# Attention scores from two float32r parts on half-height array tiles, with a new order inside the group

## The reference

```python
x = x + lru(layernorm(x))
z = layernorm(x)
h = z + attention(rmsnorm(z), wq, wk, wv, wo)   # 16 heads of 8, 1024 keys, no mask
h = h + moe(rmsnorm(h), gate, w1, w2, w3)       # 8 experts, best 2
x = x + h
```

## Time and profile before

| | |
|---|---|
| times of three runs | 1325.18, 1336.45, 1334.33 us; median 1334.33 |
| span of the profiled execution | 1326.4 us (the page gives no own time beside it; the lowest run is 1.2 us below this span) |
| mean granted TensorE clock | 0.951 of full |
| PE busy | 1187.2 us (90%) |
| DVE busy | 1033.9 us (78%) |
| ACT busy | 721.0 us (54%) |
| POOL busy | 293.1 us (22%) |
| DMA | 34.14 MB, 26 GB/s over the span |

### The profile page before, as it was taken

How to read it: one execution, slowest core, us unless ns; L and a number is a source line. 1 busy time by engine, 2 the same in 40 slices (tenths; PEclk the granted TensorE clock), 3 DMA queues, 4 the chain that set the end, 5 groups by cost and what they waited for, 6 DMA issues and landing times.

```text
span 1326.4 us, 26291 instructions
## 1 busy us (share of the span) xinstructions
PE 1187.2 (90%) x6720; PEld 583.9 (44%) x6720; DVE 1033.9 (78%) x2390; ACT 721.0 (54%) x1330; POOL 293.1 (22%) x154
## 2 busy tenths in 40 slices
PE   0266769999998999999998998999998999999998
PEld 0145522332332332332332332233335898888887
DVE  5977768888887887887887887789844677777675
ACT  1022322776776776776776776677785333333332
POOL 8133114222312222222122132132221101110100
PEclk9778866999998999999999999899999999999999
DMA  5002250011011011011011011011000000000000
GB/s 178 0 20 60 61 122 0 1 37 38 7 30 37 0 36 37 0 36 37 0 36 38 0 36 37 0 36 36 1 1 1 9 2 8 8 8 8 8 2 15
DMA packets 19748, 34.14 MB, mean 26 GB/s; under 512 B 4417, under 2 KB 13889, under 8 KB 16961
## 3 DMA queue, kind: packets, MB, share of 16 engines
q1 hardware_dynamic: 17456, 32.52, 10.7%
q10 hardware_dynamic: 2192, 0.66, 0.2%
HBM read 24.78 MB, written 8.39 MB: 25 GB/s over the span
## 4 chain that ended last, share of the span: by engine, by line
PE 78%; DVE 10%; issue 6%; DMA 3%; SPq 1%; ACT 1%; POOL 1%; DVEq 0%; POOLq 0%; ACTq 0%
PE ps L923 18%; PE ps L976 16%; PE ps L966 15%; PE ps L1126 13%; PE ps L1114 9%; DMA qpack<-q_parts 2%; PE ps L911 2%; DVE smax L670 2%; SPq L238 1%; DVE wk L624 1%; DMA xacc<-x 1%; PE ps L984 1%; PE ps L995 1%; PE ps L899 1%; POOL qpack L293 1%
## 5 line engine op out<-in xcount | busy, mean ns | idle before, releaser
L670 DVE TENSOR_REDUCE smax<-ps 128x1 f32<-128x512 f32 x1024 | 654.1, 686 | 104.9 <-PE ps L923 77.7
L462 ACT ACTIVATE prob<-ps 128x512 f32<-128x512 f32 x1024 | 537.3, 600 | 223.3 <-PE ps L966 200.4
L923 PE MATMUL ps<-kpack,qpack 96*128 96x512 bf16 x1024 | 365.4, 397 | 32.2 <-DVE smax L670 28.3
L966 PE MATMUL ps<-qpack,kpack 96*128 96x512 bf16 x1024 | 350.5, 385 | 1.5 <-ACT prob L462 1.5
L976 PE MATMUL ps<-prob,vpad 128*32 128x512 f32 x2048 | 278.0, 615 | 0.1
L923 PEld LDWEIGHTS ps<-kpack,qpack 96*128 96x128 bf16 x1024 | 100.2, 98 | 372.7 <-DVE smax L670 296.0
L293 POOL TENSOR_TENSOR qpack<-mtr,mdiag 12x2048 bf16<-12x2048 bf16 x32 | 129.9, 4058 | 585.8 <-ACT mtr L455 585.8
L1126 PE MATMUL ps<-split_parts 128*128 (+1 forms) x768 | 208.7, 407 | 0.0
L519 ACT ACTIVATE prob<-ps 128x512 f32<-128x512 f32 x128 | 76.6, 599 | 182.4 <-PE ps L1126 181.4
L851 DVE TENSOR_TENSOR prob<-ps,prob 128x512 f32<-128x512 f32 x128 | 87.9, 691 | 85.3 <-PE ps L1126 72.8
L1126 PEld LDWEIGHTS ps<-split_parts 128*128 128x128 f32 x768 | 135.0, 189 | 22.3
(11 more groups left out here) (154 smaller groups left out, 665.0 us busy)
## 6 DMA issues: line engine op xcount, KB each, us to landing
kpack<-k_parts SPq DMA_DIRECT2D x48, 192.0 KB
qpack<-q_parts SPq DMA_DIRECT2D x144, 64.0 KB
w<-w_t SPq DMA_DIRECT2D x3, 1024.0 KB, 10.1
q_parts<-qk SPq DMA_DIRECT2D x48, 64.0 KB, 1.6
k_parts<-qk SPq DMA_DIRECT2D x48, 64.0 KB, 1.6
xacc<-x SPq DMA_DIRECT2D x4, 512.0 KB, 7.9
out<-xacc SPq DMA_DIRECT2D x8, 256.0 KB, 2.3
gam<-gamma_row ACTq DMA_DIRECT2D x1, 64.0 KB, 5.5
```

Of the source, the lines that this page charges most:

```text
L462: act.activation(prob[:, v % RING, :], bank(3 + v % 3), ACT.Exp).then_inc(exp_done, 1)
L670: dve.tensor_reduce(smax[:, half, w // 2, w % 2:w % 2 + 1], bank(6 + u % 2 if opening else u % 3), AX_X, ALU.max).then_inc(s_max, 1)
L923: pe.matmul(bank(6 + u % 2 if opening else u % 3), qpack[:, slot, head, q0:q0 + P], kpack[:, slot, head, kh * 512:(kh + 1) * 512], start=T ...
L966: pe.matmul(bank(3 + v % 3), kpack[:, slot, head, kt * P:(kt + 1) * P], qpack[:, slot, head, half * HALF:(half + 1) * HALF], start=True, s ...
```

## The change

- q and k are split in two float32r parts (`PARTS = 2`) instead of three bf16 parts: ACT writes the high part straight from PSUM, DVE the rest as (PSUM times scale minus high), also from PSUM. Four cross products are 32 contraction rows; 2 rows hold the maxima: 34 partitions.
- Heads of even number lie on partitions 0 to 33, those of odd number on 64 to 97. A row *pair* is two matmuls, one of each half, into two neighbouring banks; one reduction takes the maxima of both. Pairs alternate between banks 0, 1 and 2, 3. The turned output takes one position of this rotation (O), the turned maxima one of the column rotation (banks 4 to 6). Values are in bank 7.
- In a group: both row pairs, four columns, values of the group before, then (where due) output turn and maxima turn.
- Maxima are split in two steps of float32r with nothing between them, turned by one transpose, and placed by two small DMAs on SP's queue instead of by POOL. POOL's clear becomes two memsets.
- Loads of a quad: 4 for k, 16 for q; 8 of the latter already after half the columns of the quad that held the slot.
- `front` staging of the first block uses banks 2 and 3; PE waits for the split before it overwrites the banks of q and k.

```diff
-PARTS = 3
-MROWS = PARTS * (HALF // P)
-PAIR0 = 24
-ROWS = PAIR0 + PARTS * PARTS * HD
+PARTS = 2
+CROSS = PARTS * PARTS * HD
+ROWS = CROSS + PARTS
+ODD = 64
+        def row_banks(pos):
+            return 2 * (pos % 2)
+        def col_bank(pos):
+            return 4 + pos % 3
...
 (sync: loop)
-                    sp.wait_ge(st_done, i * (2 * UNITS) + (slot + 1) * UNITS)
-                    load_pack(2 * i + 2 + slot, slot)
+                    sp.wait_ge(col_free, base + (M_OWN + 1))
+                    place_maxima(slot, 1)
+                    sp.wait_ge(col_full, base + (col_pos(JOB - 1) + 1))
+                    load_q(n, slot, 0)
+                    sp.wait_ge(col_free, base + (M_NEXT + 1))
+                    place_maxima(1 - slot, 0)
+                    sp.wait_ge(col_full, base + (col_pos(UNITS - 1) + 1))
+                    load_k(n, slot)
+                    load_q(n, slot, 1)
...
 (scalar: projections)
-                    act.activation(full, bank(2 + 2 * w, 2), ACT.Copy, scale=(scale, 1.0)[w]).then_inc(qk_saved, 1)
-                    act.activation(qk3[:, w, 0, :], full, ACT.Copy).then_inc(hi_ready, 1)
-                    act.activation(qk3[:, w, 1, :], (q_rest, k_rest)[w], ACT.Copy).then_inc(mid_ready, 1)
+                    act.activation(qk2[:, w, 0, :], bank(2 + 2 * w, 2), ACT.Copy,
+                                   scale=(scale, 1.0)[w]).then_inc(hi_ready, 1)
...
 (vector)
-                    dve.tensor_reduce(smax[:, half, w // 2, w % 2:w % 2 + 1], bank(6 + u % 2 if opening else u % 3), AX_X,
-                                      ALU.max).then_inc(s_max, 1)
+                    dve.tensor_reduce(smax[:, half, :, pair, qt, kh], ps[:, first:first + 2, :], AX_X,
+                                      ALU.max).then_inc(row_free, 1)
...
 (tensor: rows; `pos` is the place in the rotation)
+                    pe.wait_ge(row_free, base + (pos - 1))
+                for par in range(2):
+                    r = par * ODD
+                    ins = pe.matmul(bank(first + par), qpack[r:r + ROWS, slot, half, pair, qt * P:(qt + 1) * P],
+                                    kpack[r:r + ROWS, slot, pair, kh * HALF:(kh + 1) * HALF], start=True, stop=True)
+                ins.then_inc(row_full, 1)
...
 (tensor: columns)
-                    pe.wait_ge(exp_done, base + (2 + max(v - 2, 0)))
+                        pe.wait_ge(col_free, base + (pos - 2))
+                    pe.matmul(bank(col_bank(pos)), kpack[r:r + ROWS, slot, head // 2, kt * P:(kt + 1) * P],
+                              qpack[r:r + ROWS, slot, half, head // 2, :],
+                              start=True, stop=True).then_inc(col_full, 1)
...
 (tensor: turn of the output)
+                pe.wait_ge(row_free, row_item - 1)
                 for t in range(4):
+                    ins = pe.transpose(ps[:, o_bank, t * P:(t + 1) * P], oT[:, t * P:(t + 1) * P], ident[:, :])
+                ins.then_inc(row_full, 1)
...
 (tensor: group)
-                rows(0, 1)
-                score_cols(4 * g, 4 * g + 2, slot, units)
-                rows(1, 3)
-                score_cols(4 * g + 2, 4 * g + 3, slot, units)
-                rows(3, 4)
-                (turn_o, turn_maxima where due)
-                score_cols(4 * g + 3, 4 * g + 4, slot, units)
-                weigh_values(g - 1, slot, units)
+                rows(0)
+                rows(1)
+                score_cols(4 * g, 4 * g + 4, slot, cols, not has_next)
+                weigh_values(g - 1, slot, cols, not has_next)
+                (turn_o, turn_maxima where due)
```

More of the change, by code:

```diff
@@ L275, in _ @@
[L275 to L283, removed]
@@ L687, in _ @@
             norm_a(chain(0), B - 1)
-            dve.sem_inc(s_max, 4)
-            split_qk(B - 1, between=lambda: maxima(0, AHEAD, 0, opening=True))
+            split_qk(B - 1)
             assert count[0] == start + B * PER_BATCH, count[0]
             start += B * PER_BATCH
-            dve.sem_inc(o_done, 1)
             dve.sem_inc(hid_done, 2)
             dve.sem_inc(added, 2)
-            def split_maxima(job, half, units, before, first=False, beside=None):
-                done = [0]
-                def step(ins):
-                    ins.then_inc(dve_self, 1)
-                    if beside:
-                        maxima(beside[0] + done[0], beside[0] + done[0] + 1, beside[1])
-                    done[0] += 1
-                    dve.wait_ge(dve_self, before + done[0])
-                dve.wait_ge(s_max, units + 4)
-                if not first:
-                    dve.wait_ge(m_turned, job)
-                negated, rest = (nmax[:, i, :].rearrange("p (h t) -> p h t", h=HQ) for i in range(2))
-                step(dve.tensor_reduce(nmax[:, 0, :], smax[:, half, :, :], AX_X, ALU.max, negate=True))
-                step(dve.tensor_copy(mpart[:, :, 0, :], negated))
-                step(dve.tensor_tensor(rest, negated, mpart[:, :, 0, :], ALU.subtract))
-                step(dve.tensor_copy(mpart[:, :, 1, :], rest))
-                dve.tensor_tensor(mpart[:, :, 2, :], rest, mpart[:, :, 1, :], ALU.subtract).then_inc(m_split, 1)
@@ L723, in finish_o @@
+            def finish_o(quad, half, full, o_bank, before):
+                dve.wait_ge(row_full, full)
+                o = bank(o_bank).rearrange("p (g c) -> p g c", c=VW)
                 dve.reciprocal(rden[:, :], o[:, :, HD]).then_inc(dve_self, 1)
@@ L794, in first_front @@
                 assert count[0] == PER_BLOCK, count[0]
-            PER_QUAD = 10
-            maxima(AHEAD, JOB, 0, opening=True)
-            split_maxima(0, 0, JOB, start, first=True)
-            maxima(JOB, UNITS - LAG + 4 * START, 0)
-            start += 4
+            PER_QUAD = 6
+            maxima(0, 16, 0, opening=True)
+            split_maxima(0, 16, start)
+            maxima(16, PAIRS - 2, 0, opening=True)
+            start += 2
             def dve_quad(i, slot, last):
-                units = i * (2 * UNITS) + slot * UNITS
-                job, quad = 4 * i + 2 * slot, 2 * i + slot
+                base = i * (2 * ROW_ITEMS) + slot * ROW_ITEMS
+                quad = 2 * i + slot
@@ L805, in dve_quad @@
                 own = i * (2 * PER_QUAD) + (slot * PER_QUAD + start)
-                maxima(UNITS - LAG + 4 * START, UNITS, units)
-                following = units + UNITS
-                split_maxima(job + 1, 1, following, own, beside=None if last else (0, following))
+                following = base + ROW_ITEMS
+                maxima(PAIRS - 2, PAIRS, base)
+                split_maxima(1, base + (pair_pos(PAIRS - 1) + 1), own)
                 if not last:
-                    maxima(4, 28, following)
@@ L811, in dve_quad @@
-                finish_o(quad, 0, job, own + 4)
-                if not last:
-                    maxima(28, JOB, following)
-                    split_maxima(job + 2, 0, units + (UNITS + JOB), own + 5, beside=(JOB, following))
-                    maxima(JOB + 4, UNITS - LAG + 4 * START, following)
-                    finish_o(quad, 1, job + 1, own + 9)
-                else:
-                    first_front(own + 5)
-                    finish_o(quad, 1, job + 1, own + (5 + PER_BLOCK))
+                    maxima(0, 14, following)
@@ L896, in first_half @@
                 pe.wait_ge(uT_saved, b + 1)
+                if not first:
+                    pe.wait_ge(lo_ready, b * 2)
                 for i in range(2):
@@ L913, in product_y, with score_rows @@
                 ins.then_inc(y_done, 1)
[L915 to L925 removed]
+            def score_rows(p, slot, base, opening=False):
+                pos = pair_pos(p, opening)
+                half, pair, qt, kh = p // 16, p % 16 // 8, p % 8 // 2, p % 2
+                first = (6 - 2 * (p % 2)) if opening and p < 16 else row_banks(pos)
+                if not opening or p >= 2:
+                    pe.wait_ge(row_free, base + (pos - 1))
+                for par in range(2):
+                    r = par * ODD
+                    ins = pe.matmul(bank(first + par), qpack[r:r + ROWS, slot, half, pair, qt * P:(qt + 1) * P],
+                                    kpack[r:r + ROWS, slot, pair, kh * HALF:(kh + 1) * HALF], start=True, stop=True)
+                ins.then_inc(row_full, 1)
             def second_half(b, has_next):
@@ L951, in second_half @@
                     pe.wait_ge(v_saved, b + 1)
-            first_half(0)
+            first_half(0, first=True)
             product_y(0)
@@ new lines, in group @@
+                rows(0)
+                rows(1)
+                score_cols(4 * g, 4 * g + 4, slot, cols, not has_next)
+                if g == 0:
+                    if not opening:
+                        weigh_values(15, 1 - slot, cols - COL_ITEMS)
+                else:
+                    if g == 1:
+                        pe.wait_ge(vpad_in, quad + 1)
+                    if g % 8 == 1 and not (opening and g == 1):
+                        pe.wait_ge(o_saved, job + g // 8)
```

(1 more changed line is left out.)

388 lines of the change are left out of this document (208 added, 180 removed).

## The result

The changed kernel takes 1715.1 us (median of four runs, 1699.8 to 1716.2) against 1331.9 us before: 1.282 times as long, 95% interval 1.274 to 1.290. I had forecast 1362 us. The direction was right, the size and its cause were not.

What follows compares the result with a forecast made beforehand. PE was taken as the bound, DVE close. Terms +22 + 1 + 20 - 6 - 3.5 - 7 = +26.5, say +28 us, put on the 1334.3 us median: 1362 us; forecast 1345 to 1390, range 1322 to 1410.

Steps and rivals of the forecast that it cites:

- rival 4: TensorE's clock falls with idle time: +1.8 us a group over a fifth of the groups, about 1450 us; chance 0.03.
- My argument against the rival: Old kernel's last quad: groups of 2.40 us, idle share like the one expected, kept matmul spacing at 0.22.
- The group at 2.4 GHz: Plain attention group: 2.40 + 0.46 + 0.07 = 2.93 us against 2.84, +22 us over 244 groups.
- The chain: Column 0, exponential 0.44 us later, column 3 after 0.64, values after 0.32, next column 0 after 1.00: 2.40 us every group.
- 0.07 for loads: Weight loads on PE, after the values and at column 3, not wholly hidden: 0.07 us a group.
- Row pairs: Row matmuls of a group: the two halves run at the same time, 0.46 us, bounds 0.43 and 0.93.
- rival 1: Row halves do not run together, or their loads go one after the other: 1477 or 1438 us; chance 0.14.
- Maxima: DVE's two reductions of 1024 a group: 2.4 to 2.5 us, under PE's time, costed at nothing.
- Loads: PE's waits for loads at the end of a quad, 3.5 us in all before, go: -3.5 us.
- The turned output: Output turn in the row rotation: PE waits for DVE's division, 0.65 us about 31 times, +20 us.
- The turned maxima: Four transposes become one after the values: -0.2 us x 31 = -6 us, bounds 0 and -10.
- Opening: Before the first columns: 16 paired reductions replace 28, start 0.4 us earlier; -7 us, first columns near 211 us.

Runs made afterwards that it cites:

- the padded kernel: The changed kernel with all score matmuls over 64 contraction rows instead of 34, added rows zeros in q and ones in k: 1384.8 us, 1.040 of before.
- experiment 3: Changed kernel, score matmuls over 64 contraction rows instead of 34 (zeros in q, ones in k), order untouched: 1384.8 us, 1.040 of before.
- experiment 4: Kernel before (bf16, 96 rows) with only the order in a group changed, so that PE waits: 1397.3 us, 1.049 of before.
- experiment 8: Kernel before, order and bf16 kept, score matmuls over the first 34 of 96 contraction rows, output not the reference's: 1610 and 1686 us.
- experiment 2: Changed kernel with the values of the group before moved in front of column 3: 1591 and 1593 us, 1645 in two other runs; 1.195 of before.
- experiment 1: Changed kernel with alternating order: row pair, columns 0 and 1, row pair, columns 2 and 3, values: 1458 and 1521 us, no ratio given.

## Why the prediction was wrong, step by step

**The clock** was the step that failed. I had it as rival 4 with a chance of 0.03, about 1450 us, over a fifth of the groups, and brought on by idle time. The sum itself put the change from 96 to 34 contraction rows at nothing, without a reason. The runs show that this change cost most: its price is the difference to the padded kernel, the same list of instructions, 1715 - 1385 = **330 us** of the 383 lost, with a group of 5.00 us at the lower level instead of my 4.7. At 5.00 - 3.16 = 1.84 us a group, 330 us are about 180 of the 256 groups; this is an estimate. My argument against the rival, that the last quad of the old kernel kept its clock with the same idle share, was right about the waits (experiments 3 and 4), but those matmuls had 96 rows. At one level of the clock the narrow matmuls show no difference: at 2.4 GHz four row matmuls take 0.58 us over 34 rows and over 64 alike (604.61 - 604.03).

Idle time is not without effect. In the kernel before, PE stood still for 3.92 us at a turn of the loop, and the clock went down (stretches as above, then the first row unit after the standstill):

```profile
420.00:425.00 5.00, 1.25 (x6) 0.39 (x4) 0.71 (x2) 1.55 (x3) 0.00 (x0) 0.91 0.12 21
425.00:430.00 5.00, 4.83 (x15) 1.12 (x16) 2.94 (x8) 1.47 (x4) 0.00 (x0) 0.50 0.00 2
430.00:435.00 5.00, 5.00 (x32) 1.52 (x30) 4.37 (x10) 3.30 (x7) 0.00 (x0) 0.91 0.00 0
```

```profile
425.17 0.61 PE L923 MATMUL ps<-kpack,qpack 96*128 96x512 bf16 x1 [3.92 <-DVE smax L670]
```

With 96 rows it was back up soon after 430 us. In experiment 8, the same kernel over 34 rows, it went down behind a standstill of the same kind (PE busy for 2.2 us of 350 to 355) and stayed down until about 530.

**The group at 2.4 GHz.** Forecast 2.93 us, measured 3.16. The chain is the one I gave, column 3 waits in every group, but three terms were too small: rows 0.58 for 0.46, column 0 to its exponential 0.51 for 0.44, column 3 to the values 0.42 for 0.32. Exponential to column 3 (0.65) and the values (1.00) were right. I had allowed 0.07 for loads; the gap behind column 3 grew by 0.10, and its load takes 0.18 us there. That the load causes it was not tested.

**Row pairs** run together (rival 1 false). **Maxima**: the new reduction takes 1.22 us, DVE idle 0.6 to 0.8 us a group; right, and costs nothing. **Loads**: in the changed kernel PE waits for none any more; right.

**The turned output.** In the changed kernel at the full clock the values before and after a turn lie 605.49 - 601.11 = 4.38 us apart, 1.22 more than a plain group; 0.44 of it was paid before. So +0.78 us for a forecast +0.65.

**The turned maxima.** Their group takes 0.21 us more than a plain one (561.80 - 558.43 = 3.37), half of what it was: -0.2, right. **Opening**: first columns at 208.75 us instead of 218.51: -10 for a forecast -7.

**Missed: the loop's turn.** Before, DVE stood still at turns of the loop with nothing to wait for, PE with it, and the clock dropped for some us after it, as shown above. DVE's waits for nothing but issue (us in total, times, longest), before and in the changed kernel:

```profile
DVE smax L670 <- issue: 22.8, 6, 4.3
```

```profile
DVE smax L715 <- issue: 0.4, 2, 0.2
```

POOL's clears give the length of the quads: before, they lie 53.95 and 48.12 us apart in turn (410.09, 464.04, 512.16), over twelve quads 50.2 us on average (265.39 to 868.33; the longer of each two 52.9, the shorter 47.6); in the padded kernel 53.36 us each, so 3.1 us more. By steps: 16 x 0.32 = +5.1, turns 2 x 0.78 = +1.6, maxima -0.4, and the loop's turn -5.3 in two quads, -2.6: together +3.7, an estimate that leaves 0.6 us open. DVE's shorter list (1806 instructions for 2390) goes with the missing stall; that it is the cause was not tried.

**The time without the clock.** By the two profiles the padded kernel is 61 us longer than the kernel before (by the medians 53). From the first values to the last it takes 857.9 us instead of 784.9, +73; the way to the first values is 12.5 us shorter (211.4 instead of 223.9). Of the 73, some 47 are fifteen quads at 3.1 us; the rest was not taken apart, but the padded kernel comes up from the lower clock later (in 230 to 240 us, against 220 to 230) and drops to it once more for some 15 us after 1054 us.

So without the loss of clock the kernel would have been 4% slower, at 1385 us. That this lies inside my range is partly luck. The group alone costs 244 x 0.32 = 78 us for my 22, and the turn of the loop, which I had not seen, gives back six times 5.3 = 32. The mechanism I had named, column 3 and the row pairs uncovered, is there, but its size was off by more than three times, and it is no part of the 330 us.

## What to carry to other kernels

Here matmuls with few contraction rows took no less time at the same clock, and cost the clock. When a change narrows the contraction (packing, fewer parts, two heads on half tiles), read the granted clock of a stretch before anything else, and try rows of zeros up to the full height of the tile: here that was worth 330 us, and at the upper clock a group took 3.16 us with them and without. And count the list of each engine between two uses of a bank: an order that puts three independent matmuls together and the dependent fourth behind them needs something else in the gap. The values in the gap took the padded kernel from 1385 to 1278 us.

## What the runs showed of the hardware

- With 34 contraction rows TensorE's clock stayed at 1.2 GHz in 430 to 530 us, with PE busy for 99.7 and 100 of 100 us (experiments 2 and 8). With 64 rows in each half it stayed at 2.4 GHz there with PE idle for 17% (experiment 3), and with 96 rows it was 0.98 of full with PE idle for 7% (experiment 4). Zeros serve as well as ones.
- At 34 and 48 rows both levels occur within one run, in stretches with the same list of instructions. At 34 rows one lasted for over 800 us at the lower level (experiment 2) and one for 200 us at the upper (experiment 1, 830 to 1030 us). The order alone moved the mean over 210 to 1030 us: 0.61 in the changed kernel, 0.77 alternating, 0.50 with the values in the wait. What changes the level at a given moment was not explained: one fall followed a turn of the output with 0.38 us of waiting, but the turns of other groups passed without one.
- After a standstill of PE of 3.92 us the clock was at 1.2 GHz in 425 to 430 us; with 96 rows it was back up soon after 430 (kernel before).
- A reduction over two PSUM banks, 1024 elements, took 1.22 us against 2 x 0.63 for two single ones.
- Two halves of the rows: four matmuls of 512 columns in float32r took 0.58 us, over 34 rows and over 64 (the changed kernel, experiment 3).
